# Layer 1's scores by four 64-row and four 128-row matmuls, all ahead of the transposes and the weighing

## The reference

```
h      = einsum('bnc,hdc->bhnd', x1, Wh)            # 4 heads, D = 64
scores = einsum('...nd,...md->...nm', h, h)         # 2048 x 2048 per batch and head
attn   = softmax(where(mask, scores, -1e16))
out_h  = einsum('...nm,...md->...nd', attn, h) + b
z      = leaky_relu(concat over heads, 0.2)
h2     = z @ Wo.T ; the same attention on h2, one head ; leaky_relu ; layer norm
```

## Time and profile before

| what | us |
|---|---|
| median of 3 runs (lowest to highest) | 3392.47 (3391.7 to 3395.71) |
| profiled execution | 3385.7 |
| its span, first to last instruction | 3384.0 |
| PE matmul busy | 3073.0 (91%) |
| DVE busy | 2755.6 (81%) |
| POOL busy | 2600.1 (77%) |
| ACT busy | 2336.7 (69%) |

### The profile page before, as it was taken

One profiled execution on the slowest core, in us unless ns is written; L12 is line 12 of the kernel. 1 busy time (PEld: TensorE's weight loads), 2 busy tenths in 40 slices (PEclk: granted clock), 3 DMA queues, 4 the chain that ended last, 5 costly groups with the idle time before them and its releaser, 6 DMA issues. The chain is left out here.

```text
span 3384.0 us, 126835 instructions
## 1 busy us (share of the span) xinstructions
PE 3073.0 (91%) x49399; PEld 2298.0 (68%) x49399; DVE 2755.6 (81%) x5040; ACT 2336.7 (69%) x2678; POOL 2600.1 (77%) x1891
## 2 busy tenths in 40 slices
PE   4874679999999999999999999999996599999997
PEld 3433457777777777777777777777765477777775
DVE  5477668888888888888888888888876599999998
ACT  1003557777777777777777777777765488888886
POOL 1026968999999999999999999999986337676775
PEclk7886989999999999999999999999998899999998
DMA  5103679998999999899999999999976623333331
GB/s 204 64 0 124 233 172 159 174 178 161 163 181 171 162 178 176 163 172 179 167 166 175 174 163 175 178 161 167 180 135 202 207 105 142 125 139 130 142 127 72
DMA packets 1195556, 528.52 MB, mean 156 GB/s; under 512 B 1091998, under 2 KB 1149788, under 8 KB 1192988
## 3 DMA queue, kind: packets, MB, share of 16 engines
q1 hardware_dynamic: 1193964, 518.57, 73.0%
q0 software_dynamic: 1200, 3.93, 0.3%
HBM read 123.09 MB, written 62.91 MB: 55 GB/s over the span
## 5 line engine op out<-in xcount | busy, mean ns | idle before, releaser
L627 POOL TENSOR_TENSOR mask_slot<-probs 128x1024 f16<-128x1024 f32 x1024 | 1915.7, 1893 | 209.5 <-ACT probs L984 123.0
L984 ACT ACTIVATE probs<-scores,shifted_max 128x2048 f32<-128x2048 f32 x512 | 1026.1, 2004 | 171.2 <-DVE shifted_max L1191 167.3
L1186 DVE CUSTOM_DVE_ANT_0 scores<-ps,mask 128x1024 f32<-128x1024 f32 x512 | 627.1, 1225 | 259.9 <-PE ps L842 255.3
L841 PE MATMUL ps<-operands 128*128 128x512 f16 x2048 | 778.7, 380 | 15.8 <-DMA v_parts<-h_d 15.1
L842 PE MATMUL ps<-operands 128*128 128x512 f16 x2048 | 778.0, 380 | 0.0
L989 ACT COPY probsT<-ps 128x1024 bf16<-128x1024 bf16 x512 | 518.1, 1012 | 360.9 <-PE ps L850 360.9
L1186 DVE CUSTOM_DVE_ANT_0 scores<-ps,mask,neg_max 128x1024 f32<-128x1024 f32 x512 | 657.4, 1284 | 93.3 <-issue 66.3
L850 PEld LDWEIGHTS ps<-ident,probs 128*128 128x128 bf16 x8192 | 515.8, 98 | 283.8 <-issue 145.9
L850 PE MATMUL ps<-ident,probs 128*128 128x128 bf16 x8192 | 624.2, 219 | 6.8 <-DVE probsT L1195 4.9
L861 PE MATMUL ps<-v_parts,probsT 128*128 128x64 f16 x8192 | 547.6, 193 | 0.0
L860 PE MATMUL ps<-v_parts,probsT 128*128 128x64 f16 x8192 | 547.2, 193 | 0.0
(11 more groups left out here) (171 smaller groups left out, 4640.1 us busy)
## 6 DMA issues: line engine op xcount, KB each, us to landing
mask_slot<-mask SPq DMA_DIRECT2D x129, 512.0 KB, 2.9
operands<-hT_d SPq DMA_DIRECT2D x160, 256.0 KB, 4.1
operands<-hT_d SPq DMA_DIRECT2D x40, 512.0 KB, 4.7
v_parts<-h_d SPq DMA_DIRECT2D x40, 512.0 KB, 5.0
scores<-in_adj SPq DMA_DIRECT2D x16, 1024.0 KB, 4.8
h_d<-outs SPq DMA_DIRECT2D x32, 512.0 KB, 2.8
hT_d<-probs SPq DMA_DIRECT2D x32, 512.0 KB, 2.8
probsT<-mask_slot SPq DMA_TRANSPOSE x1024, 3.9
```

The costliest lines, as they stand in the source:

```text
L627: pool.tensor_tensor(low[:, u, w], probs[:, u, w], high[:, u, w], ALU.subtract).then_inc(sem(f"low{half}"), 1)
L841: pe.matmul(ps[:, b, :], k_both[:, p, t * P:(t + 1) * P], q_head[:, p, w], start=True, stop=False)
L984: act.activation(probs[:, 1 - u, :], scores[:, 1 - u, :], ACT.Exp, bias=shifted_max[:, 1 - u:2 - u], scale=-1.0, accum_out=row_sum[:, held ...
L1186: dve.tensor_tensor_reduce(scores[:, u, w], ps[:, 2 * c:2 * c + 2, :].rearrange("p a n -> p (a n)"), mask[:, t * N + c * 2 * BANK:t * N + ...
```

## The change

The third operand buffer is no longer used for operands. `hi_lo` is what `k_both` was: high parts in rows 0 to 63, low parts in rows 64 to 127. `lo_hi` has them the other way round. Four DMAs per instance fill them: one of 128 rows, two of 64, and `v_parts`.

In layer 1 the product of high with high parts is computed by one 64-row matmul per block: blocks 0 and 2 from rows 0 to 63 of `hi_lo`, blocks 1 and 3 from rows 64 to 127 of `lo_hi`. Then four 128-row matmuls of `hi_lo` with `lo_hi` add high with low and low with high. The product of low with low parts is left out in layer 1. All eight stand together, behind waits for both halves of the tile before; then come all sixteen transposes, then the low-part weighing, then the high-part weighing. The half's semaphore is raised after the second and the fourth of the 128-row matmuls. In layer 2 the two matmuls per block read `hi_lo` with `hi_lo` and `hi_lo` with `lo_hi`, 128 rows as before. The loads of the next instance take four steps of SP instead of six.

```diff
-OPERAND_DMAS = 6
+OPERAND_DMAS = 4
...
-                to, half, part, rows_ = ((q_head, 0, 0, D), (q_tail, 0, 1, D), (k_both, 0, 0, P), (q_head, 1, 0, D), (q_tail, 1, 1, D))[k]
-                at = i * P + part * D
-                sp.dma_start(to[half * D:half * D + rows_, parity, :],
+                to, row, at, rows_ = ((hi_lo, 0, 0, P), (lo_hi, 0, D, D), (lo_hi, D, 0, D))[k]
+                at = i * P + at
+                sp.dma_start(to[row:row + rows_, parity, :],
...
                 if live and t == 0:
                     pe.wait_ge(sem(f"operands{p}"), (i - p) * (8 * OPERAND_DMAS) + 16 * OPERAND_DMAS)
+                if live:
+                    for half in range(2):
+                        since(pe, sem(f"masked{half}"), g)
+                    for b in range(4):
+                        both, rows_ = ((hi_lo, slice(0, D)), (lo_hi, slice(D, P)))[b % 2]
+                        pe.matmul(ps[:, b, :], both[rows_, p, t * P:(t + 1) * P], both[rows_, p, b * BANK:(b + 1) * BANK],
+                                  start=True, stop=False)
+                    for b in range(4):
+                        scored = pe.matmul(ps[:, b, :], hi_lo[:, p, t * P:(t + 1) * P], lo_hi[:, p, b * BANK:(b + 1) * BANK],
+                                           start=False, stop=True)
+                        if b % 2 == 1:
+                            scored.then_inc(sem(f"scores{b // 2}"), 1)
+                if turning:
+                    pe.wait_ge(sem("exp_done"), g - 1)
+                    for half in range(2):
+                        since(pe, sem(f"high_copied{half}"), g - 2)
+                        for j in range(8):
+                            key = (8 * half + j) * P
+                            flipped = pe.transpose(high_bank(half)[:, j * P:(j + 1) * P], high[:, u, key:key + P], ident16[:, :])
+                        flipped.then_inc(sem(f"turned{half}"), 1)
                 if back(4):
                     old, held, tt = back(4)
                     for c in range(NT):
...
                     added.then_inc(sem("weighed"), 1)
-                for half in range(2):
-                    if live:
-                        since(pe, sem(f"masked{half}"), g)
-                        for b in (2 * half, 2 * half + 1):
-                            w = slice(b * BANK, (b + 1) * BANK)
-                            pe.matmul(ps[:, b, :], k_both[:, p, t * P:(t + 1) * P], q_head[:, p, w], start=True, stop=False)
-                            scored = pe.matmul(ps[:, b, :], k_both[:, p, t * P:(t + 1) * P], q_tail[:, p, w], start=False, stop=True)
-                        scored.then_inc(sem(f"scores{half}"), 1)
...
```

More of the change, by code:

```diff
@@ L74, in build @@
         operands = sb("operands", [P, 3, 2, N], F16)
-        q_head = operands[:, 0]
-        q_tail = operands[:, 1]
-        k_both = operands[:, 2]
+        hi_lo = operands[:, 0]
+        lo_hi = operands[:, 1]
         v_parts = sb("v_parts", [P, 2, NT * P], F16)
@@ L93, in build @@
         h_lo = operands[:, 0:2].rearrange("p a u n -> p (a u n)")
-        shifted = k_both[:, 0, 0:2 * BD]
+        shifted = operands[:, 2, 0, 0:2 * BD]
         a_in = v_parts[:, :, :].rearrange("p u n -> p (u n)").bitcast(F32)
@@ L258, in within @@
             return not isinstance(k, int) or 0 <= k < UNITS
-        ones16 = k_both[:, 1, 0:P]
+        ones16 = operands[:, 2, 1, 0:P]
         TURN_BANK = (4, 5, 6, 5)
@@ L427, in load_part @@
                 s = sem(f"operands{parity}")
-                if k == 5:
+                if k == 3:
                     sp.dma_start(v_parts[:, parity, :], h_d[:, i, :] if isinstance(i, int) else h_d[:, bass.ds(i, 1), :]).then_inc(s, 16)
                     return
-                to, half, part, rows_ = ((q_head, 0, 0, D), (q_tail, 0, 1, D), (k_both, 0, 0, P), (q_head, 1, 0, D), (q_tail, 1, 1, D))[k]
-                at = i * P + part * D
-                sp.dma_start(to[half * D:half * D + rows_, parity, :],
+                to, row, at, rows_ = ((hi_lo, 0, 0, P), (lo_hi, 0, D, D), (lo_hi, D, 0, D))[k]
+                at = i * P + at
+                sp.dma_start(to[row:row + rows_, parity, :],
                              hT_d[at:at + rows_, :] if isinstance(i, int) else hT_d[bass.ds(at, rows_), :]).then_inc(s, 16)
@@ L764, in half @@
                         w = slice((2 * c + q) * BANK, (2 * c + q + 1) * BANK)
-                        k = col(k_both[:, parity], t, P)
-                        pe.matmul(o, k, q_head[:, parity, w], start=True, stop=False)
-                        last = pe.matmul(o, k, q_tail[:, parity, w], start=False, stop=True)
+                        k = col(hi_lo[:, parity], t, P)
+                        pe.matmul(o, k, hi_lo[:, parity, w], start=True, stop=False)
+                        last = pe.matmul(o, k, lo_hi[:, parity, w], start=False, stop=True)
                     last.then_inc(sem(f"l2_scores{c}"), 1)
```

## The result

The changed kernel takes 3463.03 us (median of 4 runs, 3462.48 to 3464.63) beside 3392.09 for the kernel before: a ratio of 1.0209, 95% interval 1.0191 to 1.0227. It is slower by 71 us. I had forecast 3420, with a range up to 3475: the sign was right, the size 2.5 times too small. The profiled execution has a span of 3462.9 against 3384.0, so 78.9 us are to be found in the two traces.

What follows compares the result with a forecast made beforehand. TensorE bounded layer 1 at 4.02 us a tile; the change makes a ring of 4.16: 511 x 4.16 + 5 = 2131, less 2097, +34, less 6 is +28 on the median 3392.47: 3420 us, range 3346 to 3475.

Steps and rivals of the forecast that it cites:

- DVE's signal to the next score matmul: Layer 1, from DVE's half 1 minimum written to TensorE's next score matmul: 0.06 us, read at the layer's start.
- the stalls left in layer 1: Of some 41 us of stalls beyond layer 1's 511 regular tiles, 5 us would remain; ends 0 and 41.
- TensorE's own tile: TensorE's work per layer 1 tile: 4.02 us before, bounding the layer; 3.59 after the change saves 0.43.
- the ring: Layer 1: scores wait for both masked halves, DVE waits for scores; 4.02 us, 4.16 a tile with the switch of shape.
- the four terms: Scores to DVE's half 0 1.25, to half 1 1.40, to its minimum 1.29, signal to next scores 0.06 us.
- DVE's tail: DVE's minimum shift and highT copy after half 1 run beside the next scores, ending 0.4 us before those are ready.
- The pairs: Layer 1's 64-row score matmuls on opposite row halves run side by side, one slot of 0.215 us per pair.
- The rival of pairs in turn: 64-row matmuls of a pair run one after the other: 4.59 us a tile, 3640 us; chance 11%.
- The switch of shape: Last 64-row to first 128-row score matmul in layer 1: 0.14 us extra per tile, ends 0.00 and 0.20.
- The rival of a free switch: Changing from 64-row to 128-row matmuls costs nothing at 2.4 GHz: 4.03 us a tile, 3354 us; chance 27%.
- Late transposes: DMA transposes issued later in layer 1 slip POOL's start by 0.2 us, cost 0; as rival +90, 3510 us, chance 10%.
- The heads: Starts of both layers: two operand loads fewer per instance save 1.9 and 3.8 us, 6 in all; ends 0 and 8.

Runs made afterwards that it cites:

- same rows: The changed kernel with all four 64-row matmuls on the upper 64 rows of hi_lo, so no pair on opposite rows; 3682.1 us.

## Why the prediction was wrong

Two terms of the sum were too small, and their steps failed: DVE's signal to the next score matmul (0.06 taken, 0.147 measured) and the stalls left in layer 1 (5 taken, 38 measured, 25 of them at back edges that the prediction did not have).

*TensorE's own tile and the ring.* Right: TensorE bounded the kernel before, and the 0.43 saved turned into idle time. That the four terms add up to the tile shows nothing by itself, since they follow each other from one tile's scores to the next; in the kernel before, where TensorE sets the tile, they add up to 4.033 as well, with 0.08 for the last. What shows the ring are the edits: 0.09 less of signal gave a tile shorter by 0.092, pairs in turn gave one longer by 0.413 although TensorE had 0.35 to spare, and one pair taken from behind the signal gave one shorter by one slot (4.125 to 3.910). DVE's tail, which was to end 0.4 ahead of the next half (the earlier trace rows give 0.5), ends 0.70 ahead and has no part in it.

*The pairs.* Right: side by side, second matmul 0.006 behind the first. The rival of pairs in turn would have been 4.63, and "same rows" shows it.

*The switch of shape.* 0.14 taken, 0.104 measured, 0.04 too much. The scaling of the setup's figures to 2.4 GHz held; the late weights added nothing beyond it. The rule that changing the tiling mode drains the engine (the Trainium skill, "TensorEngine Tiling (Array Packing)", Key Properties) agrees with both directions, 0.097 and 0.104. The rival of a free switch falls.

*DVE's signal to the next score matmul.* The term of the sum that was mis-sized: 0.06 taken, 0.147 measured, 0.09 x 511 = 46 us. I had taken it from a place where TensorE waits for one signal. The change waits for two, and of two waits ahead of one matmul one becomes an instruction; here it is the late one. The prediction named what stands behind the wait, but not how many waits there are. With one wait the tile is 4.125.

*The ring* was then 1.364 + 1.413 + 1.292 + 0.147 = 4.216 instead of 4.16: 0.057 x 511 = 29 us more. That 4.217 still lies within the forecast's own 4.09 to 4.22 is luck: the upper edge stood for a switch of 0.20, and the switch taken too long hid part of the signal taken too short.

*The stalls left in layer 1.* 5 us taken, 38 measured. The old stalls, mostly late DMA transposes, did go, as said: with one wait the rest is 14. In their place came a cost that no step of the prediction had, the back edges: 13 x 1.92 = 25 us, and the tiles right behind them. The wait that became an instruction lengthened TensorE's program by one instruction per tile.

*Late transposes.* The cost of 0 was right, the sign given for it wrong: POOL's wait on the DMA transposes well over 100 us was to show the forecast wrong, and it is 206.8 without setting the tile. With one wait it is still 173 and the time is gone; with the weighing moved back it is 63.4 and the time is longer. The move of the low-part weighing was worth some 20 us to the good, by the experiment that undoes it.

*The heads.* -6 taken, -17 measured outside layer 1. The load's bytes at the first head's rate were too little (3.2 instead of 1.9, and 5.4 less of DVE's wait instead of 3.8).

Sum: +28, + 29 for the tile, + 33 for the rest, - 11 for the heads = +79, the difference of the spans. The change as such is not slow: with one wait it is level with the kernel before, and with the wait split it is 2.5% faster.

## What to carry to other kernels

When an edit makes an engine wait where it did not, add up the ring that this closes, and count the waits: two ahead of one instruction can put one of them, as an instruction of its own, between the late signal and the work. Place behind the late signal only what needs it: moving one pair of matmuls ahead of it and giving each wait its own carrier was worth some 150 us here, 25 of them at the back edges. And compare the branch at the loop's end and the number of instruction fetches before the tile is explained: one more instruction per tile, in an unrolled loop, cost 25 us and more without doing anything.

## What was unexpected of the hardware

- A wait that is an instruction of its own between signal and matmul: 0.147 from DVE's write to TensorE's start instead of 0.057. A wait long true costs nothing where TensorE does not wait: tile 4.034 against 4.031.
- The back edge of TensorE's long loop takes 0.36 or 2.0 to 3.3 us, by where some tens of instructions lie, with one more packet in the instruction queue each time.
- At 2.4 GHz, a switch from 64 to 128 rows costs 0.104 and one back 0.097; a pair of 64-row matmuls on opposite rows takes one slot of 0.215.
